# Cross-attention and FFN: the product with V' moved next to the scores, and the engines' orders laid out anew

## The reference

```python
def xattn(q, k, v, Wq, Wk, Wv, Wo, bo, mask):            # 16 heads of 64
    qh, kh, vh = split_heads(q @ Wq), split_heads(k @ Wk), split_heads(v @ Wv)
    dots = einsum('bhid,bhjd->bhij', qh, kh) * SCALE      # masked, causal
    out = einsum('bhij,bhjd->bhid', softmax(dots), vh)
    return merge_heads(out) @ Wo + bo
x = x + xattn(layernorm(x), ctx, ctx, ...)
x = x + ffn(layernorm(x))       # gate = silu(bitlinear), up = bitlinear, bitlinear(gate * up)
```

## Time and profile before

| | us |
|---|---|
| median of 3 runs | 822.8 (821.91 to 822.95) |
| the profiled execution | 821.9 |
| its span, first to last instruction | 820.1 |
| PE busy | 783.2 (96%) |
| DVE busy | 678.8 (83%) |
| ACT busy | 678.9 (83%) |
| Pool busy | 407.3 (50%) |

### The profile page before, as it was taken

One profiled execution on the slowest core, in us unless ns is written; L12 is line 12 of the kernel. 1 busy time (PEld: TensorE's weight loads), 2 busy tenths in 40 slices (PEclk: granted clock), 3 DMA queues, 4 the chain that ended last, 5 costly groups with the idle time before them and its releaser, 6 DMA issues.

```text
span 820.1 us, 17819 instructions
## 1 busy us (share of the span) xinstructions
PE 783.2 (96%) x5487; PEld 542.6 (66%) x5550; DVE 678.8 (83%) x1845; ACT 678.9 (83%) x1202; POOL 407.3 (50%) x404
## 2 busy tenths in 40 slices
PE   7899999999999999999999999999999999999983
PEld 5667666766766766676666676676676667666552
DVE  7749888888878887988888888788888888878894
ACT  4688888888888887988888888788888888888882
POOL 1235555454554545555545545555454554544551
PEclk9999999999999999999999999999999999999997
DMA  7100010100101000010100101010010100000000
GB/s 225 53 1 1 15 38 16 39 2 14 40 14 39 13 18 22 13 39 13 38 2 13 39 13 38 14 39 0 13 39 14 39 13 13 1 14 15 1 14 14
DMA packets 37109, 20.50 MB, mean 25 GB/s; under 512 B 1460, under 2 KB 36534, under 8 KB 37046
## 3 DMA queue, kind: packets, MB, share of 16 engines
q1 hardware_dynamic: 37046, 19.84, 8.3%
HBM read 15.64 MB, written 4.19 MB: 24 GB/s over the span
## 4 chain that ended last, share of the span: by engine, by line
PE 81%; DVE 8%; issue 5%; ACT 4%; POOL 1%; DMA 0%; DVEq 0%; POOLq 0%; ACTq 0%
PE ps_s L431 13%; PE ps_a L500 12%; PE ps_s L402 5%; PE ps_s L322 4%; PE ps_kv L402 3%; PE ps_kv L322 3%; PE ps_s L324 3%; PE ps_kv L323 3%; PE ps_s L323 3%; PE ps_s L404 3%; PE ps_b L459 3%; PE ps_s L403 3%; PE ps_a L459 3%; PE ps_kv L403 3%; PE ps_kv L324 3%
## 5 line engine op out<-in xcount | busy, mean ns | idle before, releaser
L872 POOL TENSOR_TENSOR prob<-prob,row_max 128x1024 f32<-128x1024 f32 x64 | 122.0, 1906 | 189.4 <-DVE row_max L747 189.4
L520 ACT ACTIVATE vp<-ps_s 64x512 f32<-64x512 f32 x256 | 151.2, 590 | 33.2 <-PE ps_s L404 28.9
L890 POOL TENSOR_TENSOR prob<-prob,row_rec 128x512 f32<-128x512 f32 x128 | 130.9, 1044 | 56.3 <-DVE row_rec L822 56.3
L520 ACT ACTIVATE vp<-ps_kv 64x512 f32<-64x512 f32 x256 | 151.5, 592 | 5.4
L882 POOL TENSOR_TENSOR hid_b<-hid_q,neg_round 128x512 bf16<-128x512 f32 x64 | 66.7, 1041 | 128.1 <-DVE hid_q L791 128.1
L500 PE MATMUL ps_a<-vp,prob_t 128*64 128x128 f32 x2048 | 125.9, 276 | 1.3 <-DVE x L769 1.2
L431 PE MATMUL ps_s<-kp,xn_t 128*64 128x512 f32 x512 | 124.0, 605 | 2.9 <-ACT vp L520 1.9
L500 PEld LDWEIGHTS ps_a<-vp,prob_t 128*64 128x64 f32 x2048 | 110.6, 137 | 24.4 <-issue 16.3
L744 DVE TENSOR_TENSOR prob<-ps_s,bias_sb 128x1024 f32<-128x1024 f32 x64 | 78.3, 1223 | 54.3 <-PE ps_s L431 53.7
L520 ACT ACTIVATE kp<-ps_s 128x512 f32<-128x512 f32 x130 | 77.8, 599 | 11.9 <-PE ps_s L290 8.2
L849 POOL TENSOR_TENSOR rs<-ve,neg_half 128x1 f32<-128x1 f32 x128 | 70.4, 550 | 33.1 <-DVE ve L669 24.5
(11 more groups left out here) (175 smaller groups left out, 1725.5 us busy)
## 6 DMA issues: line engine op xcount, KB each, us to landing
x_in<-in_x SPq DMA_DIRECT2D x16, 256.0 KB, 2.9
ctx_in<-in_ctx SPq DMA_DIRECT2D x16, 256.0 KB, 3.4
x_res<-in_x SPq DMA_DIRECT2D x16, 256.0 KB, 2.8
out<-x SPq DMA_DIRECT2D x15, 256.0 KB, 2.4
kp<-in_L_xattn_Wk SPq DMA_DIRECT2D x1, 512.0 KB, 4.0
kp<-in_L_xattn_Wq SPq DMA_DIRECT2D x1, 512.0 KB, 4.9
kp<-in_L_xattn_Wv SPq DMA_DIRECT2D x1, 512.0 KB, 6.1
kp<-in_L_xattn_Wo SPq DMA_DIRECT2D x1, 512.0 KB, 6.1
```

Source lines behind the costliest of these rows:

```text
L520: copy = lambda dst, src, **kw: nc.scalar.activation(dst, src, ACT.Copy, **kw)
L872: p.tensor_tensor(prob[c % 2][:], prob[c % 2][:], rows(row_max[c % 2]), ALU.subtract).then_inc(shifted, 1)
L890: p.tensor_tensor(prob[c % 2][:, heads, :], prob[c % 2][:, heads, :], rows(row_rec[c % 2])[:, heads, :], ALU.mult).then_inc(normed, 1)
```

## The change

The whole of the attention product moves one slot back: pair s-2 instead of s-1, as the first thing in TensorE's slot, with the scores of pair s right behind it (both address the array in column halves). The steps behind it on VectorE move along, so the second layer norm is that of pair s-2, in the same slot as its gate and up. Around it the orders are new:

- TensorE: attention product, scores, v0, transposes of hid_b, k0, v1, down-projection (now into ps_g), k1, transpose of xq, both halves of prob's transposes, v2, gate and up, k2, k3, in a group's second slot the transposes of x, v3, in its last those of the context. The PSUM banks of the quarters are the same in all slots (`V_BANK`, `K_BANK`).
- ScalarE: follows TensorE's order; take_v(2) stands ahead of tanh, exp behind it.
- VectorE: residual and second layer norm first, with the bias addition between them; the row maximum; x2; `ln1_apply`; gated to clip; row sum; the reciprocals; hid_q.
- Pool: hid_b (pair s-3) and the second rstd come at the slot's start, ahead of the subtraction; before they stood behind the subtraction and ahead of the normalising products.

```diff
+                if live(it, c, 2):
+                    pe.wait_ge(pt_evac, 2 * s - 2)
+                    pe.wait_ge(v_evac, 8 * s - 8)
+                    if x_turn(it, c - 1):
+                        pe.wait_ge(xnt_evac, g + 2)
+                    for a in range(HP):
+                        for b in range(2):
+                            t = mm(ps_a[b * S:(b + 1) * S, 0:D], prob_t[:, a, b * S:(b + 1) * S],
+                                   vp[c % 2][:, b, a, :], start=(a == 0), stop=(a == HP - 1))
+                    t.then_inc(attn_ready, 1)
...
                     if live(it, c, 1):
-                        pe.wait_ge(v_evac, 8 * s - 2)
                         if not isinstance(it, int) or group_ahead(it, c - 1, 1):
-                            pe.wait_ge(k_evac, 16 + 4 * s - 1)
+                            pe.wait_ge(k_evac, 16 + 4 * s)
+                        else:
+                            pe.wait_ge(v_evac, 8 * s - 4)
...
-                early = q == 0 and group_ahead(it, c, 1)
-                if early:
-                    v_quarter(0)
-                if live(it, c, 2):
-                    if live(it, c, 3):
-                        pe.wait_ge(h_step, H_STEPS * (s - 3) + 2)
-                    pe.wait_ge(xq_ready, s - 1)
-                    nc.tensor.transpose(ps_x, xq[:], id_sb[:]).then_inc(xqt_ready, 1)
-                if live(it, c) and q == 0 and group_ahead(it, c, 1):
+                v_quarter(0)
+                if makes_k and q == 0:
                     pe.wait_ge(ctlo_ready, g + 2)
-                    pe.wait_ge(xnt_evac, g + 2)
                 if live(it, c, 3):
                     pe.wait_ge(hb_ready, s - 2)
                     for k in range(FB):
                         t = nc.tensor.transpose(ps_h[:, k * P:(k + 1) * P], hid_b[:, k * P:(k + 1) * P], id_bf[:])
                     t.then_inc(ht_ready, 1)
+                k_quarter(0)
+                v_quarter(1)
+                if live(it, c, 3):
+                    pe.wait_ge(ht_evac, s - 2)
+                    for k in range(FB):
+                        t = mm(ps_g[:, 0:D], hid_t[:, k, :], wd_t[:, k, :], start=(k == 0), stop=(k == FB - 1))
+                    t.then_inc(down_ready, 1)
+                k_quarter(1)
+                if live(it, c, 2):
+                    pe.wait_ge(xq_ready, s - 1)
+                    nc.tensor.transpose(ps_x, xq[:], id_sb[:]).then_inc(xqt_ready, 1)
...
@@ -466,53 +488,31 @@
...
                     prob_transposes(0, ps_a)
+                    pe.wait_ge(normed, 2 * s)
+                    prob_transposes(1, ps_b)
+                v_quarter(2)
                 if live(it, c, 2):
                     pe.wait_ge(xqt_evac, s - 1)
+                    if live(it, c, 3):
+                        pe.wait_ge(x2_done, s - 2)
...
-                if not early:
-                    v_quarter(0)
-                if live(it, c, 1):
-                    pe.wait_ge(normed, 2 * s)
-                    if live(it, c, 3):
-                        pe.wait_ge(ht_evac, s - 2)
-                    prob_transposes(1, ps_b)
-                k_quarter(0)
...
-                v_quarter(1)
-                k_quarter(1)
-                if live(it, c, 1):
-                    pe.wait_ge(pt_evac, 2 * s)
-                    pe.wait_ge(v_evac, 8 * s)
-                    if live(it, c, 3):
-                        pe.wait_ge(x2_done, s - 2)
-                    for a in range(HP):
-                        for b in range(2):
-                            t = mm(ps_a[b * S:(b + 1) * S, 0:D], prob_t[:, a, b * S:(b + 1) * S],
-                                   vp[(c - 1) % 2][:, b, a, :], start=(a == 0), stop=(a == HP - 1))
-                    t.then_inc(attn_ready, 1)
-                v_quarter(2)
                 k_quarter(2)
                 k_quarter(3)
+                if x_turn(it, c):
+                    pe.wait_ge(xn_ready, GP * g + 2 * GP)
+                    pe.wait_ge(pt_evac, 2 * s - 1)
+                    transpose_x(1 - par)
                 v_quarter(3)
                 if live(it, c) and q == GP - 1 and group_ahead(it, c, 2):
                     pe.wait_ge(ctx_loaded[par], 16 * (it + 2))
-                    pe.wait_ge(xn_ready, GP * g + 3 * GP)
-                    pe.wait_ge(x1_done, s)
+                    pe.wait_ge(pt_evac, 2 * s)
...
@@ -599,36 +599,33 @@
                 if first(it, c):
                     rest_of_setup()
+                take_v(0)
+                if live(it, c, 3):
+                    act.wait_ge(ht_ready, s - 2)
+                    copy(flat(hid_t[:, :, :]), ps_h[:, :]).then_inc(ht_evac, 1)
+                take_k_quarter(0)
+                take_v(1)
+                take_k_quarter(1)
                 if live(it, c, 2):
                     act.wait_ge(xqt_ready, s - 1)
                     copy(xq_t[:], ps_x, bias=-ROUND).then_inc(xqt_evac, 1)
-                if live(it, c, 3):
-                    act.wait_ge(ht_ready, s - 2)
-                    copy(flat(hid_t[:, :, :]), ps_h[:, :]).then_inc(ht_evac, 1)
                 take_probs(0, ps_a)
+                take_probs(1, ps_b)
+                take_v(2)
...
-                if group_ahead(it, c, 1):
-                    take_v(0)
-                    take_probs(1, ps_b)
-                else:
-                    take_probs(1, ps_b)
-                    take_v(0)
-                take_k_quarter(0)
-                take_v(1)
                 if live(it, c) and not first(it, c):
                     exponential(s, c)
-                take_k_quarter(1)
-                take_v(2)
                 take_k_quarter(2)
                 take_k_quarter(3)
+                if x_turn(it, c):
+                    take_x(1 - par, g + 1)
                 take_v(3)
                 if live(it, c) and q == GP - 1 and group_ahead(it, c, 2):
                     take_ctx(par, g + 2)
-                    take_x(par, g + 2)
...
                 if live(it, c):
-                    dve.wait_ge(exp_done, s + 1)
-                    v.tensor_reduce(row_sum[:], prob[c % 2][:], AX, ALU.add).then_inc(sum_step, 1)
...
-                    dve.wait_ge(rstd2_done, s)
+                    dve.wait_ge(scores_ready, s + 1)
+                    pair_bias = bias_sb[:, s:s + 1, :] if isinstance(it, int) else bias_sb[:, bass.ds(s, 1), :]
+                    v.tensor_tensor(prob[c % 2][:], ps_s[:, :].rearrange("p (h j) -> p h j", j=S),
+                                    pair_bias.broadcast_to([P, H, S]), ALU.add).then_inc(biased, 1)
...
+                if ffn:
+                    dve.wait_ge(rstd2_done, s - 1)
...
+                if ahead:
+                    ln1_stats(par, q, s + BODY, 16 * (it + 2) if q == 0 else None)
+                    dve.wait_ge(ln1_step, LN1_STEPS * (s + BODY) + 1)
+                if live(it, c):
+                    dve.wait_ge(biased, s + 1)
+                    v.tensor_reduce(row_max[c % 2][:], prob[c % 2][:], AX, ALU.max).then_inc(max_done, 1)
+                if ahead:
+                    ln1_aggregate(s + BODY)
+                if live(it, c, 3):
+                    dve.wait_ge(h_step, H_STEPS * (s - 2))
+                    dve.wait_ge(down_ready, s - 2)
+                    e = (c - 3) % BODY
+                    o = x1[e // GP][:, e % GP, :]
+                    v.scalar_tensor_tensor(o, ps_g[:, 0:D], o_scale[:, e % 4:e % 4 + 1], o,
+                                           ALU.mult, ALU.add).then_inc(x2_done, 1)
+                if ahead:
+                    ln1_apply(par, q, s + BODY)
+                if ffn:
+                    dve.wait_ge(tanh_done, s - 1)
+                    v.scalar_tensor_tensor(gated[:], tanh_sb[:], 1.0, ps_g[:, :], ALU.add, ALU.mult).then_inc(h_step, 1)
...
+                if live(it, c):
+                    dve.wait_ge(exp_done, s + 1)
+                    v.tensor_reduce(row_sum[:], prob[c % 2][:], AX, ALU.add).then_inc(sum_step, 1)
+                if ffn:
+                    dve.wait_ge(h_step, f + 4)
+                    v.reciprocal(rec3[:], clip3[:]).then_inc(h_step, 1)
+                if live(it, c):
+                    dve.wait_ge(sum_step, 2 * s + 1)
+                    v.reciprocal(row_rec[c % 2][:], row_sum[:]).then_inc(sum_step, 1)
...
+                    dve.wait_ge(h_step, f + 6)
+                    if live(it, c, 3):
+                        dve.wait_ge(hb_ready, s - 2)
+                    v.tensor_scalar(hid_q[:], hid[:], qs3[:], ROUND, ALU.mult, ALU.add).then_inc(hq_ready, 1)
...
@@ -867,6 +860,15 @@
                 rows = lambda t: t[:].rearrange("p (h o) -> p h o", o=1).broadcast_to([P, H, S])
                 if live(it, c) and q == 0:
                     residual(par, 2 * it + par, 16 * (it + 1))
+                if live(it, c, 3):
+                    pool.wait_ge(hq_ready, s - 2)
+                    if live(it, c, 4):
+                        pool.wait_ge(ht_ready, s - 3)
```

(54 more changed lines are left out.)

92 lines of the change are left out of this document (29 added, 63 removed).

## The result

The changed kernel takes **1017.9 us** (median of 4 runs, 1013.9 to 1018.7) where the kernel before takes 822.9 (4 runs on the same chip, 821.9 to 823.0): a ratio of 1.236, interval 1.233 to 1.240. The prediction had said slower, which holds, and 950 us with a range of 890 to 985, which does not. The profiled run took 1013.9 us; its span is 1012.1.

What follows compares the result with a forecast made beforehand. TensorE, 96% busy, was taken to bound the kernel before; afterwards a 13.65 us ring against 11.66 costs 2.0 us in 63 turns, 126, plus 2: span 948, forecast 950 us, range 890 to 985.

Steps and rivals of the forecast that it cites:

- The clock: Rival: TensorE, newly idle, falls to half pace at each of 15 group starts; +67, 1017 us; chance 0.06.
- term 6: Last part of ring one: row_sum to row_rec 1.24, to Pool 0.34, normalisation halves 2.04, hid_b 1.04 us.
- ring one: Loop from Pool's hid_b through TensorE, ScalarE, VectorE and Pool's normalisation back to hid_b; 13.65 us a slot.
- the path to the V' copy: From the end of Pool's hid_b through TensorE's work to the start of take_v(2); 4.73 us.
- The worth of the join: On TensorE, product with V' directly ahead of scores saves one leaving and one entering: 0.31 us a slot, 19 us.
- terms 1 to 3: Pool to TensorE 0.08, TensorE from hid_b's transposes through v_quarter(2) 4.45, result delay 0.2; sum 4.73 us.
- Ring two: Loop of VectorE and Pool alone from row_max to row_max, with xn's bare 1.9 us wait for Pool's rstd; 13.3 us.
- shortening one ring alone would give little: Claim that the VectorE and Pool loop, 13.3 us, is nearly as long as the one through TensorE, 13.65.
- The residual at a group's start: Pool's residual ahead of hid_b in each group's first slot: 1.27 us against 1.28 before, so no difference.
- The gap of 3.65 us: TensorE's wait for xq in the kernel before, read as standing at full clock before the last slice.

Runs made afterwards that it cites:

- e2_hb: Changed kernel with hid_q ahead of the row sum on VectorE and hid_b ahead of the normalisation on Pool, same slot's pair; 967.4 us.
- e3_both: e2_hb and e1_xn edits together on the changed kernel, xn standing between clip3 and its reciprocal; 966.0 us.
- e1_xn: Changed kernel with VectorE's ln1_apply (xn) alone moved behind clip3, ahead of the row sum; 1032.2 us.
- e11_join: Kernel before, product with V' moved to slot end ahead of next scores in three slots of four, row sum ahead of x1; 1086.7 us.
- e8_best: e3_both plus second rsqrt between normalisation halves, first row maximum before setup, x2 before row maximum, gate, up and tanh before third V' quarter and copy; 904.2 us.

## Why the direction was right and the size wrong

Two steps failed. The clock was held to be safe, and its falls cost some 29 us; term 6 of ring one and the path to the V' copy were too small, 22 us. Slot 0, which was not looked at, adds 5.7. Ring one itself, its order and its releases, is as predicted.

- **The worth of the join** (19 us at 0.31 a slot) nearly stands: 0.24 to 0.32 measured, and TensorE did wait instead of saving it.
- **Ring one** stands as a mechanism, term by term. Too small were the path to the V' copy (terms 1 to 3: 4.73 forecast, 4.94 from 412.93 to 417.87) and term 6: the normalisation takes 2.23 us with hid_q beside it, where the earlier trace rows had 2.04. Together, with what small differences are left, 14.00 instead of 13.65: 0.35 in 63 turns, 22 us.
- **hid_q beside the normalisation** was not weighed at all. By the lines of VectorE, before and after:
```profile
L791 DVE TENSOR_SCALAR hid_q<-hid,qs 128x512 f32<-128x512 f32 x64 | 30.8, 481 | 0.5 <-DVE qs L783 0.2
```
```profile
L832 DVE TENSOR_SCALAR hid_q<-hid,qs 128x512 f32<-128x512 f32 x64 | 82.3, 1287 | 2.3
```
  0.48 us became 1.29, which is the 52 of the 54 us that VectorE is busier. In the slot before the one shown, Pool's first half starts at 409.70 and its second at 410.70; hid_q starts at 409.72 and ends at 411.03, 0.3 us into the second half. The Trainium skill's page "SBUF — State Buffer", Who interferes with whom, has VectorE and GpSimd share one pair of ports under an exclusive lock, which VectorE's tensor_scalar can take; by that rule the one that comes second waits until the other's instruction has ended, and the trace agrees: in e2_hb and e3_both, where hid_q runs with Pool idle, it is back at 0.49.
- **Ring two** was sized right in its wait (1.88 for 1.9), and "shortening one ring alone would give little" held for it (e1_xn). For ring one it held less well: its cut took 0.78 us off the turn, and with the clock it gave 50 us. A third ring of 13.2 us was missed; it set no time in the kernel after, but it is why cutting both gave no more.
- **The residual at a group's start** was put at no difference, 1.27 against 1.28. It adds 1.21 us to the ring in each group, and the slot in which x is transposed adds 0.30, so the step was short by 0.2 us a group, 3 us. By the starts of the scores a group of four takes 58.84 or, with the loop's jump, 60.63 us after and 47.94 before; four turns of 14.00 and these two make 57.51. What is beyond is the clock, and at a jump some 0.6 us more.
- **The clock** was a rival with a chance of 0.06, and its time of 1017 is the one measured, but by accident: it assumed a fall only at group starts and 4.5 us lost at each, 67 us. There were one or two falls in nearly every group, 23 in turns of the ring, at about 1.3 us each: 29 us. The step that failed is the reading of the earlier trace rows with the earlier trace rows. The gap of 3.65 us was taken to stand before the slice with the lower clock, as a sign that idle stretches of 2 to 3 us are safe. It stands inside that slice (each is 20.5 us, the last begins at 799.6), and the clock fell 0.3 us behind it, by the timeline's windows of the kernel before:
```profile
804.20:807.80 3.60, 0.00 (x0) 0.01 (x1) 2.73 (x13) 0.00 (x0) 1.59 (x2) 1.00 0.00 0
808.20:812.00 3.80, 1.71 (x9) 0.60 (x6) 2.11 (x4) 1.52 (x3) 0.00 (x0) 0.50 0.07 20
```
- **Slot 0** was missed, 5.7 us: the setup of V' on VectorE now stands ahead of the first row_max, and TensorE waits behind its consequences (the kernel after's timeline):
```profile
42.11 1.90 POOL L874 TENSOR_TENSOR prob<-prob,row_max 128x1024 f32<-128x1024 f32 x1 [13.56 <-DVE row_max L793]
...
45.73 0.77 PE L324 MATMUL ps_kv<-ct_hi,m_hi 128*128 128x512 f32 x1 [5.23 <-ACT wd_t L520]
```
Sum: 22 + 29 + 5.7 + 3 = 60 us, and the span came out 64 us above the forecast 948. The terms are no better known than that: the pipeline's filling and draining and what the loop's jumps cost beyond those of the kernel before are in none of them.

## What to carry to other kernels

When a change lays out several engines' orders anew, follow one result round all of them until it feeds its own start; the longest such ring is the slot, whatever each engine's busy share says. Then look for the next ring before promising what cutting one brings. And a TensorE that newly idles two or three microseconds in every slot should be priced at the lower clock too. Whether an idle stretch was harmless is read from the clock of the few microseconds behind it, not from a row of slices of 20 us.

## What the runs showed of the hardware

- In the kernel after, where TensorE is 81% busy, 27 of the 29 falls to 1.2 GHz began in, or less than 2 us behind, an idle stretch of 2.1 to 3.5 us ahead of hid_b's transposes. The kernel before, 96% busy, fell once, 0.3 us behind its idle stretch of 3.65 us. Not every such stretch brought a fall: the turn after the idle 2.18 us at 412.98 ran at full clock.
- Filling the idle time with useless matmuls made the kernel 12 us faster (1017.9 to 1005.5).
- Leaving the column-tiled stretch and entering it again cost TensorE 0.24 to 0.32 us.
- VectorE beside Pool's normalisation: hid_q 0.48 to 1.29 us, xn2 0.25 us to 1.05 in e11_join, and the normalisation 2.04 to 2.23.
- Ahead of ct_lo at each jump of the loop VectorE stands still with no releaser in the profile: 2.6 to 2.9 us in the kernel before, 1.7 to 1.8 in the kernel after, 2.7 to 2.8 in e8_best. The cause was not tested.
